# A convolution in fp16 halves: another order of the prologue, and the folds of unit 2 two streams earlier

## Chip, cores and metric

One core of one Trainium2 chip. The time is the device time of one execution in microseconds (us); lower is better. TensorE is called PE, VectorE DVE, ScalarE ACT, GpSimd POOL; SyncE is SP and only issues DMAs.

## What is computed

The input x has 32 images of 32 channels, 56 by 56 points, in float32. Each channel of each image is normalised by itself, then convolved with a 7 by 7 filter that is built from nine weighted points for each pair of channels; the bias and x itself are added.

```python
def construct_kernel(weight, P):            # weight (O, Cg, 9), P (2, Cg, 9)
    ph = clip(P[0], -3, 3) + 3;  pw = clip(P[1], -3, 3) + 3
    ih, iw = floor(ph), floor(pw);  rh, rw = ph - ih, pw - iw
    kern = zeros((O, Cg, 7, 7))
    for di, dj, frac in corners:            # four bilinear corners
        kern = kern.at[:, cidx, ih + di, iw + dj].add(weight * frac[None])
    return kern

def _gn(v):                                 # 32 groups of 32 channels: one channel each
    return (v - mean(v)) / sqrt(var(v) + 1e-5)

out = x + conv(_gn(x), construct_kernel(weight, P), padding=3) + bias
```

## The kernel before

Two images make a unit; there are 16 units. An image lies on 128 partitions as 32 channels times four groups of rows. All five engines run a list written out by hand; they meet through semaphores, and each engine takes its own list strictly in order.

**The prologue** builds the filter. PE turns the weights (L781) and gives the row of their maxima (L784). DVE builds `diag` and `cols` for three chunks (L591, L594), and PE multiplies them: three chunks of four products, in float32, 24 instructions at L819, into the pairs of banks `ps_eo` and `ps_x`. Two folds of the moments of unit 0 (`mean(0)`, `variance(0)`, L789) and one product that spreads the scales (L811) stand among them. The two halves of the filter are scaled into `kern`, one by DVE (L626), one by ACT (L400, `take_second_filters`); DVE adds filter parts (`filter_sum`, L617), and each of five parts is split into a high fp16 part by ACT (`filter_high`, L408, counted by `whi_ready`) and the rest by DVE (`filter_low`, L622, `wlo_ready`).

PE also multiplies zeros by zeros. Eight such dummies stand at the very start (L776). Eighteen more (`mark`, L827) come once `kern` is ready; they write the pairs `ps_x` and `ps_y`, so that later products add to what lies there, and the last one raises `marked`.

**Each unit** goes through the same steps. ACT sums its two images (`sums`, L314), PE folds the sums over partitions (`mean`), DVE takes `negmean` (L458), ACT sums the squares (`squares`, L322), PE folds those (`variance`), DVE takes `var` (`spread`, L464), ACT the root (L328), POOL five small steps for scale and offset (`newton_step`, L726 to L739). ACT normalises three groups of rows (L338) and POOL the last (L750). DVE forms differences (`odd_differences`, `differences`, `second_differences`, all L467). Nine streams, in six batches, are split into high (ACT, L352) and low fp16 parts (DVE, L490). After each third of the streams POOL copies them to other partitions with four DMAs (`shift`, L720, `xs` to `xb`). PE takes the streams in order (`convolve`, L855): for each up to 12 pairs of products, one from `xs` on one half of the array and one from `xb` on the other. The first `xb` product of streams 0, 3 and 6 waits for the shift of that third.

**Before stream 3** PE waits for `m11_ready`: ACT has copied the product of stream 0 (`middle`, L358). Before streams 4 and 7 it waits for seeds: ACT writes scaled points of x into `ps_x` and `ps_y` (`seed`, L368), and products are added to them. DVE combines the banks (`outs_0` to `outs_4`, L494), SP stores.

**Loads.** SP issues units 0 to 3 at the start, eight DMAs each (ACT issues four of unit 0). The load of unit u + 4 waits until both seeds of unit u and POOL's normalising of it are done, since they read the same buffer; then the store of unit u follows on the same queue.

From unit 1 on the order repeats (`step` of each engine). Unit 0 and the work on unit 1 beside it are written out: on ACT the list from `sums(0, 0, 0)` on, on DVE the list after L625, on PE `step(..., first=True)`, which folds the sums of unit 2 before stream 6 and its squares before stream 8.

Of the kernel before, what the change touches and what calls it, by code (L numbers as in the profile page):

```python
# [44 lines left out]
def build(nc, x, weight, P, bias, out):  # L45
# [8 lines left out]
    with ctx:  # L54
# [133 lines left out]
        def loaded(r, nth):  # L188

            return LOAD * nth + (LOAD // PER if r == 0 else LOAD)  # L190
# [107 lines left out]
        def _(act):  # L298
# [62 lines left out]
            def seed(u, r, k, first=False):  # L361

                if first:
                    act.wait_ge(marked, 1)
                else:
                    act.wait_ge(combined, OUTS * (u - 1) + (4, 7)[k])
                photo = xraw[:, PER * r:PER * (r + 1), :].rearrange("p m (n k) -> p m n k", k=4)[:, :, :, k::2]
                act.activation(pair_of((ps_x, ps_y)[k]).rearrange("p (n m) k -> p m n k", m=PER), photo,  # L368
                               ACT.Copy, scale=scales[:, 2:3]).then_inc(seeded, 1)
# [21 lines left out]
            sums(0, 0, 0)  # L391
            squares(0, 0)
            root(0)
            act.wait_ge(xn_zeroed, 6)
            normalise(0, 0, first=True)

            def take_second_filters():
                act.wait_ge(kern_in_psum, 4)
                act.wait_ge(scales_ready, 1)
                act.activation(kern[:, :, :, 1, :].rearrange("p j q (r o) -> p r (j q) o", r=2),  # L400
                               ps_x[:, :, 0:256].rearrange("p r (v o) -> p r v o", o=CH),
                               ACT.Copy, scale=scales[:, 0:1]).then_inc(kern_ready, 1)

# [5 lines left out]

            take_second_filters()  # L410
            act.wait_ge(edges_zeroed, 2)
            high(0, 0, *BATCHES[0], first=True)
            high(0, 0, *BATCHES[1], first=True)
            sums(1, 1, 0)
            filter_high(0)
            filter_high(1)
            squares(1, 1)
            high(0, 0, *BATCHES[2], first=True)
# [4 lines left out]
            filter_high(3)  # L423
            high(0, 0, *BATCHES[5], first=True)
            act.wait_ge(bias_loaded, DMA)
            middle(0, first=True)
            seed(0, 0, 0, first=True)
            normalise(1, 1, first=True)
            high(1, 1, *BATCHES[0], first=True)
            filter_high(4)  # L430
            sums(2, 2, 0)
            high(1, 1, *BATCHES[1], first=True)
            seed(0, 0, 1, first=True)
            squares(2, 2)
# [18 lines left out]
        def _(dve):  # L453
# [144 lines left out]
            dve.wait_ge(wmax_row, 1)  # L598
            dve.tensor_reduce(srow[:, 0:1], ps_y[0:1, 0, 0:CH], AX.X, ALU.max).then_inc(srow_step, 1)
            dve.wait_ge(srow_step, 1)  # L600
# [18 lines left out]
            def filter_low(n):  # L619
# [4 lines left out]

            dve.wait_ge(kern_in_psum, 2)  # L625
            dve.tensor_scalar(kern[:, :, :, 0, :].rearrange("p j q (r o) -> p r (j q) o", r=2),  # L626
                              ps_eo[:, :, 0:256].rearrange("p r (v o) -> p r v o", o=CH),
                              scales[:, 0:1], None, ALU.mult).then_inc(kern_ready, 1)
            odd_differences(0, 0)
            dve.wait_ge(kern_ready, 2)  # L630
            filter_sum(0, sums4[:, 0:2], kern[:, 0::2], kern[:, 1::2])
            low(0, 0, *BATCHES[0])
            low(0, 0, *BATCHES[1])
            dve.wait_ge(filt_summed, 1)
            filter_sum(2, sums4[:, 4:5], sums4[:, 0:1], sums4[:, 1:2])
            filter_sum(1, sums4[:, 2:4], kern[:, 0:2], kern[:, 2:4])
            mean(1, 1)
            filter_low(0)
            differences(0, 0)
            second_differences(0, 0)  # L640
            filter_low(1)
            spread(1)
            low(0, 0, *BATCHES[2])
# [5 lines left out]
            low(0, 0, *BATCHES[5])  # L649
            outs_0(0)  # L650
            odd_differences(1, 1)
            differences(1, 1)
            filter_low(4)
            low(1, 1, *BATCHES[0])
            low(1, 1, *BATCHES[1])
            outs_1(0)
            mean(2, 0)
            second_differences(1, 0)
            second_differences(1, 2)
            low(1, 1, *BATCHES[2])  # L660
            spread(2)
            low(1, 1, *BATCHES[3])
# [109 lines left out]
        def _(pe):  # L772

            pe.wait_ge(zeros_built, 1)
            for n in range(8):
                pe.matmul(ps_y[:, n % 2, 0:N], zeros[:, 0:128], zeros[:, 0:N], start=True, stop=True)  # L776
            pe.wait_ge(weights_loaded, DMA)
# [5 lines left out]
            pe.wait_ge(wmax_ready, 1)  # L783
            pe.matmul(ps_y[0:1, 0, 0:CH], wmax[:, :], ident[:, :], start=True, stop=True).then_inc(wmax_row, 1)  # L784

# [14 lines left out]
            def variance(u):  # L800
                pe.wait_ge(ssq_ready, u + 1)
                pe.wait_ge(var_ready, u)
                fold_columns(0, PER)

            pe.wait_ge(ones_built, 1)
            for k in range(CHUNKS):
# [6 lines left out]
                for n in range(4):  # L813
                    if k == 0 and n == 2:
                        pe.wait_ge(eye_built, 2 * GROUPS)
                        mean(0)
                    if k == 1 and n == 3:
                        variance(0)
                    last = pe.matmul((ps_eo, ps_x)[n // 2][:, n % 2, 0:256],  # L819
                                     diag[:, k, 4 * n:4 * n + 4, :].rearrange("p g c -> p (g c)"),  # L820
                                     cols[:, k].rearrange("p v o -> p (v o)"), start=k == 0, stop=k == CHUNKS - 1)
                    if k == CHUNKS - 1:
                        last.then_inc(kern_in_psum, 1)

            def mark(n):

                return pe.matmul((ps_x, ps_y)[n // 2 % 2][:, n % 2, 0:N], zeros[:, 0:128], zeros[:, 0:N],  # L827
                                 start=True, stop=True)

            pe.wait_ge(kern_ready, 2)  # L830
            pe.wait_ge(scales_ready, 1)
            for n in range(10):
                mark(n)
            mean(1)
            for n in range(8):
                last = mark(n)
            last.then_inc(marked, 1)
            variance(1)

            def convolve(u, par, s, nth):  # L840
# [20 lines left out]
            def step(u, par, nth, stats, first=False):  # L861
                for s in range(NS):
# [6 lines left out]
                    if first:  # L869
                        if s == 6:  # L870
                            mean(2)
                        if s == 8:
                            variance(2)
                    elif stats:
                        if s == 1:
                            mean(u + 2)
                        if s == 5:
                            variance(u + 2)
                    if s == 4:
                        pe.wait_ge(seeded, 2 * u + 1)  # L880
                    if s == 6:
# [30 lines left out]
```

## Time and profile before

| | us |
|---|---|
| median of 3 runs | 320.43 |
| lowest, highest | 318.5, 322.21 |
| profiled execution | 320.76 |
| its span | 318.9 |

The span runs from the first to the last instruction of the program, and the rows below count from its start. A row of the timeline merges instructions of one kind that follow each other: start, duration, engine, line, operation, tiles, shapes, count, and in brackets the idle time of the engine before it with what ended it. Ends of matmuls are modelled and overlap, so the pace is read from starts. A float32 product is two instructions.

### The profile page before, as it was taken

How to read it: one execution, taken by the hardware profiler on the slowest of the kernel's cores; microseconds unless marked ns; L12 is line 12 of the kernel's file. 1: busy time of each engine (PE TensorE's matmuls, PEld its weight loads, DVE VectorE, ACT ScalarE, POOL GpSimd, SP SyncE). 2: the span in 40 equal slices, each digit the busy share in tenths (PEclk: the TensorE clock that was granted, in tenths of full speed). 3: DMA queues.
4: the chain of work that ended last, by engine and by line, in shares of the span. 5: the costliest groups of instructions: out<-in, count | busy, mean ns of one | idle time of the engine just before them, and what ended most of it. 6: DMA issues, size and time to landing. Idle time of an engine off the chain costs nothing.

```text
span 318.9 us, 9740 instructions
## 1 busy us (share of the span) xinstructions
PE 294.9 (92%) x3452; PEld 204.2 (64%) x3452; DVE 267.3 (84%) x357; ACT 225.8 (71%) x328; POOL 177.6 (56%) x338
## 2 busy tenths in 40 slices
PE   5996798796999999999999999999999999999990
PEld 2653575574766767777767676777766677776760
DVE  4448896989998999999998989899999899996231
ACT  3368887878877797969796979878787869570300
POOL 6034938466665849393948566565748393944000
PEclk9999999999999999999999999999999999999998
DMA  8953369579999898989998999999998948488605
GB/s 142 151 115 90 98 162 190 133 166 219 236 207 241 189 261 171 257 177 236 206 238 180 233 201 219 224 219 234 194 253 178 260 98 237 98 233 222 141 2 102
DMA packets 128255, 59.09 MB, mean 185 GB/s; under 512 B 122068, under 2 KB 122068, under 8 KB 128228
## 3 DMA queue, kind: packets, MB, share of 16 engines
q1 hardware_dynamic: 115204, 24.90, 43.2%
q0 software_dynamic: 9312, 33.04, 39.3%
q10 hardware_dynamic: 3712, 0.80, 1.4%
q8 instruction: 14, 0.23, 0.3%
q14 instruction: 13, 0.11, 0.1%
HBM read 12.88 MB, written 12.85 MB: 81 GB/s over the span
## 4 chain that ended last, share of the span: by engine, by line
PE 66%; POOL 11%; DMA 8%; DVE 6%; issue 5%; ACT 2%; DVEq 0%; POOLq 0%; ACTq 0%
PE ps_eo L855 18%; PE ps_x L855 17%; PE ps_s L855 16%; PE ps_y L855 11%; DMA xb<-xs 7%; POOL xn L750 4%; POOL xb L720 3%; PE ps_eo L819 2%; DVE d L467 1%; POOL rtmp L726 1%; PE ps_x L819 1%; DVE xs L490 1%; DMA wnat<-L_conv_weight 1%; ACT xs L352 1%; PE ps_stat L789 1%
## 5 line engine op out<-in xcount | busy, mean ns | idle before, releaser
L720 POOL DMA_DIRECT2D xb<-xs x192 | 94.4, 498 | 55.0 <-DVE xs L490 51.9
L855 PE MATMUL ps_eo<-xs,w 128*64 128x392 f16 (+1 forms) x576 | 98.7, 325 | 0.0
L855 PE MATMUL ps_eo<-xb,w 128*64 128x392 f16 (+1 forms) x576 | 98.7, 324 | 0.0
L855 PE MATMUL ps_s<-xb,w 128*64 128x392 f16 (+1 forms) x384 | 68.2, 326 | 8.5 <-DMA xb<-xs 8.4
L855 PEld LDWEIGHTS ps_eo<-xb,w 128*64 128x64 f16 x576 | 61.6, 109 | 16.6
L855 PE MATMUL ps_s<-xs,w 128*64 128x392 f16 (+1 forms) x384 | 69.5, 326 | 1.8 <-ACT m L358 1.8
L855 PE MATMUL ps_x<-xb,w 128*64 128x392 f16 x384 | 67.6, 328 | 0.0
L855 PE MATMUL ps_x<-xs,w 128*64 128x392 f16 x384 | 67.6, 328 | 0.0
L855 PEld LDWEIGHTS ps_eo<-xs,w 128*64 128x64 f16 x576 | 61.7, 109 | 8.7
L490 DVE TENSOR_TENSOR xs<-e,xs 128x900 f16<-128x900 f32 x48 | 65.5, 1364 | 1.7 <-ACT xs L352 1.5
L352 ACT ACTIVATE xs<-e 128x900 f16<-128x900 f32 x48 | 58.9, 1226 | 8.9 <-DVE e L467 8.0
L855 PEld LDWEIGHTS ps_s<-xb,w 128*64 128x64 f16 x384 | 40.9, 109 | 25.1 <-DMA xb<-xs 11.8
L855 PEld LDWEIGHTS ps_x<-xb,w 128*64 128x64 f16 x384 | 40.8, 109 | 16.2
L855 PE MATMUL ps_y<-xs,w 128*64 128x392 f16 x288 | 50.6, 328 | 0.0
L855 PE MATMUL ps_y<-xb,w 128*64 128x392 f16 x288 | 50.6, 328 | 0.0
L750 POOL TENSOR_SCALAR xn<-xraw,scale,offset 32x784 f32<-32x784 f32 x32 | 46.4, 1458 | 1.7
L855 PEld LDWEIGHTS ps_s<-xs,w 128*64 128x64 f16 x384 | 41.0, 109 | 7.0 <-ACT m L358 2.1
L338 ACT ACTIVATE xn<-xraw,offset,scale 96x784 f32<-96x784 f32 x32 | 34.5, 1128 | 14.8 <-POOL offset L739 14.8
L726 POOL TENSOR_TENSOR rtmp<-rinv 128x2 f32<-128x2 f32 x16 | 13.6, 851 | 51.8 <-ACT rinv L328 51.8
L855 PEld LDWEIGHTS ps_x<-xs,w 128*64 128x64 f16 x384 | 40.8, 109 | 2.3
L855 PEld LDWEIGHTS ps_y<-xb,w 128*64 128x64 f16 x288 | 31.2, 109 | 11.7
L467 DVE TENSOR_TENSOR e<-d 128x900 f32<-128x900 f32 x32 | 34.0, 1107 | 0.0
(91 smaller groups left out, 459.3 us busy)
## 6 DMA issues: line engine op xcount, KB each, us to landing
xb<-xs POOLq DMA_DIRECT2D x96, 168.8 KB, 4.5
xb<-xs POOLq DMA_DIRECT2D x96, 166.9 KB, 4.7
xraw<-x SPq DMA_DIRECT2D x124, 98.0 KB, 3.2
out<-result SPq DMA_DIRECT2D x124, 98.0 KB, 4.8
xraw<-x ACTq DMA_DIRECT2D x4, 98.0 KB, 4.0
out<-result ACTq DMA_DIRECT2D x4, 98.0 KB, 3.7
wnat<-L_conv_weight POOLq DMA_DIRECT2D x1, 36.0 KB, 3.5
pts<-L_conv_P POOLq DMA_DIRECT2D x2, 1.1 KB, 3.1
```

Of the source, the lines that this page charges most:

```text
L338: act.activation(xn[0:96, r % 2, :, SLOTS * m + 1:SLOTS * m + 1 + ROWS, 1:1 + SIDE // 2], image(r, m)[0:96, :].rearrange("p (n w k) -> p k ...
L352: act.activation(halves(par, 0, s, count), stream(s, par, count), ACT.Copy).then_inc(hi_ready, count)
L467: dve.tensor_tensor(o, both(x0, shift), both(x1, 0), ALU.subtract).then_inc(differenced, 1)
L490: dve.tensor_tensor(halves(par, 1, s, count), stream(s, par, count), halves(par, 0, s, count), ALU.subtract).then_inc(lo_ready, count)
L720: pool.dma_start(dst[32 * g:32 * g + 32, 0:run - line * past], src[32 * f:32 * f + 32, line * past:run]).then_inc(shifted[par][b], DMA)
L726: pool.tensor_tensor(rtmp[:, :], rinv[:, :], rinv[:, :], ALU.mult).then_inc(newton, 1)
L750: pool.tensor_scalar(xn[96:128, u % 2, :, SLOTS * m:SLOTS * m + ROWS, 1:1 + SIDE // 2], image(u % RING, m)[96:128, :].rearrange("p (n w k) ...
L789: last = pe.matmul(ps_stat[p:p + HALF, a:b], eye[:, p:p + HALF], moments[:, a:b], start=True, stop=True)
L819: last = pe.matmul((ps_eo, ps_x)[n // 2][:, n % 2, 0:256], diag[:, k, 4 * n:4 * n + 4, :].rearrange("p g c -> p (g c)"), cols[:, k].rearra ...
L855: last = pe.matmul(into[p:p + HALF, :, 0:PER * wide], w[:, n // 2, s, q, t, :], moving.rearrange("p n q m -> p n (q m)"), start=fresh and ...
```

## The change

- PE: fourteen dummies at the start instead of eight; five more after the row of maxima, ahead of the filter; that row goes to `ps_stat`, no longer to `ps_y`. The fold of the squares of unit 0 also waits until DVE has read the row (`srow_step`). After the filter come the fold of unit 1's sums, two dummies that mark `ps_x`, twelve dummies into `ps_s`, the fold of unit 1's squares, eight more dummies. The folds of unit 2 stand before streams 5 and 7.
- ACT: the two sums of unit 1 stand around the root of unit 0, and the seed of `ps_y` of unit 0 before its normalising; the seed of `ps_x` stands behind the squares of unit 1. ACT no longer scales the second filter half. The normalising of unit 1 stands before `middle(0)`, `filter_high(4)` one place later.
- DVE scales both filter halves, adds two filter sums and takes `negmean` of unit 1 before the odd differences of unit 0; some later steps change places.
- SP's list is the same; the load of unit 4 waits for the seeds of unit 0, which now come before its streams.

```diff
             sums(0, 0, 0)
             squares(0, 0)
+            act.wait_ge(x_loaded[1], loaded(1, 0))
+            act.wait_ge(folded, mean_fold(0))
+            act.activation(junk[:, 1, 0, :], image(1, 0), ACT.Identity, accum_out=xsum[:, 0:1])
             root(0)
+            act.activation(junk[:, 1, 1, :], image(1, 1), ACT.Identity, accum_out=xsum[:, 1:2]).then_inc(sum_ready, 1)
+            seed(0, 0, 1, first=True)
             act.wait_ge(xn_zeroed, 6)
             normalise(0, 0, first=True)
...
-            take_second_filters()
             act.wait_ge(edges_zeroed, 2)
             high(0, 0, *BATCHES[0], first=True)
             high(0, 0, *BATCHES[1], first=True)
-            sums(1, 1, 0)
+            squares(1, 1)
             filter_high(0)
             filter_high(1)
-            squares(1, 1)
+            seed(0, 0, 0, first=True)
             high(0, 0, *BATCHES[2], first=True)
...
+            normalise(1, 1, first=True)
             act.wait_ge(bias_loaded, DMA)
             middle(0, first=True)
-            seed(0, 0, 0, first=True)
-            normalise(1, 1, first=True)
             high(1, 1, *BATCHES[0], first=True)
-            filter_high(4)
             sums(2, 2, 0)
             high(1, 1, *BATCHES[1], first=True)
-            seed(0, 0, 1, first=True)
+            filter_high(4)
             squares(2, 2)
...
-            odd_differences(0, 0)
+            for t, pair in enumerate((ps_eo, ps_x)):
+                dve.wait_ge(kern_in_psum, 2 * t + 2)
+                dve.tensor_scalar(kern[:, :, :, t, :].rearrange("p j q (r o) -> p r (j q) o", r=2),
+                                  pair[:, :, 0:256].rearrange("p r (v o) -> p r v o", o=CH),
+                                  scales[:, 0:1], None, ALU.mult).then_inc(kern_ready, 1)
             dve.wait_ge(kern_ready, 2)
             filter_sum(0, sums4[:, 0:2], kern[:, 0::2], kern[:, 1::2])
-            low(0, 0, *BATCHES[0])
-            low(0, 0, *BATCHES[1])
             dve.wait_ge(filt_summed, 1)
             filter_sum(2, sums4[:, 4:5], sums4[:, 0:1], sums4[:, 1:2])
+            mean(1, 1)
+            odd_differences(0, 0)
+            low(0, 0, *BATCHES[0])
             filter_sum(1, sums4[:, 2:4], kern[:, 0:2], kern[:, 2:4])
-            mean(1, 1)
+            low(0, 0, *BATCHES[1])
+            differences(0, 0)
             filter_low(0)
-            differences(0, 0)
+            spread(1)
             second_differences(0, 0)
             filter_low(1)
-            spread(1)
...
-            outs_0(0)
             odd_differences(1, 1)
             differences(1, 1)
+            outs_0(0)
+            low(1, 1, *BATCHES[0])
+            mean(2, 0)
+            low(1, 1, *BATCHES[1])
             filter_low(4)
-            low(1, 1, *BATCHES[0])
-            low(1, 1, *BATCHES[1])
             outs_1(0)
-            mean(2, 0)
             second_differences(1, 0)
+            spread(2)
             second_differences(1, 2)
             low(1, 1, *BATCHES[2])
-            spread(2)
...
-            for n in range(8):
-                pe.matmul(ps_y[:, n % 2, 0:N], zeros[:, 0:128], zeros[:, 0:N], start=True, stop=True)
+            for n in range(14):
+                pe.matmul((ps_x, ps_y)[n // 2 % 2][:, n % 2, 0:N], zeros[:, 0:128], zeros[:, 0:N],
+                          start=True, stop=True)
...
+            for n in range(5):
+                pe.matmul(ps_x[:, n % 2, 0:N], zeros[:, 0:128], zeros[:, 0:N], start=True, stop=True)
...
                     if k == 1 and n == 3:
+                        pe.wait_ge(srow_step, 1)
                         variance(0)
...
+            mean(1)
             pe.wait_ge(kern_ready, 2)
             pe.wait_ge(scales_ready, 1)
-            for n in range(10):
-                mark(n)
-            mean(1)
-            for n in range(8):
-                last = mark(n)
+            for n in range(2):
+                last = pe.matmul(ps_x[:, n, 0:N], zeros[:, 0:128], zeros[:, 0:N], start=True, stop=True)
             last.then_inc(marked, 1)
+
+            def warm(count):
+                for n in range(count):
+                    pe.matmul(ps_s[:, 0:N], zeros[:, 0:128], zeros[:, 0:N], start=True, stop=True)
+
+            warm(12)
             variance(1)
+            warm(8)
...
                     if first:
-                        if s == 6:
+                        if s == 5:
                             mean(2)
-                        if s == 8:
+                        if s == 7:
                             variance(2)
...
                     if s == 4:
-                        pe.wait_ge(seeded, 2 * u + 1)
+                        pe.wait_ge(seeded, 2 if first else 2 * u + 1)
```

## Rows read from the trace of the kernel before

**Rows 1.** The page, busy tenths of PE in 40 equal slices.

```profile
PE   5996798796999999999999999999999999999990
```

**Rows 2.** Waits of PE, 0 to 70 us: total, times, longest.

```profile
PE ps_s L855 <- DMA xb<-xs: 5.1, 3, 1.9
```

**Rows 3.** Timeline of PE, where it resumes in units 1 and 2.

```profile
50.88 0.35 PE L855 MATMUL ps_s<-xb,w 128*64 128x392 f16 x1 [1.53 <-DMA xb<-xs]
...
58.77 0.35 PE L855 MATMUL ps_s<-xs,w 128*64 128x392 f16 x1 [1.77 <-ACT m L358]
...
78.49 0.35 PE L855 MATMUL ps_s<-xb,w 128*64 128x392 f16 x1 [2.45 <-DMA xb<-xs]
```

**Rows 4.** Timeline of PE, the prologue and the start of unit 0.

```profile
1.20 2.79 PE L776 MATMUL ps_y<-zeros 128*128 128x392 f16 x8 [1.20 <-DVE zeros L558]
...
7.14 0.26 PE L784 MATMUL ps_y<-ident,wmax 32*1 32x32 f32 x2
8.52 2.05 PE L819 MATMUL ps_eo<-cols,diag 96*128 96x256 f32 x4 [1.13 <-DVE cols L594]
...
12.68 1.91 PE L819 MATMUL ps_eo<-cols,diag 96*128 96x256 f32 x4
14.39 1.06 PE L819 MATMUL ps_x<-cols,diag 96*128 96x256 f32 x2
...
19.22 1.91 PE L819 MATMUL ps_x<-cols,diag 96*128 96x256 f32 x4
21.91 0.83 PE L827 MATMUL ps_x<-zeros 128*128 128x392 f16 x2 [0.78 <-ACT kern L400]
...
24.50 0.86 PE L827 MATMUL ps_x<-zeros 128*128 128x392 f16 x2
...
26.05 0.49 PE L827 MATMUL ps_y<-zeros 128*128 128x392 f16 x2
26.38 0.49 PE L827 MATMUL ps_x<-zeros 128*128 128x392 f16 x2
...
30.16 0.35 PE L855 MATMUL ps_s<-xb,w 128*64 128x392 f16 x1 [1.67 <-DMA xb<-xs]
```

**Rows 5.** Timeline of DVE, 17 to 25 us.

```profile
19.54 0.75 DVE L626 TENSOR_SCALAR kern<-ps_eo,scales 128x512 f32<-128x512 f32 x1 [1.92 <-PE ps_eo L819]
20.20 1.08 DVE L467 TENSOR_TENSOR e<-xn 128x900 f32<-128x900 f32 x1
21.89 0.69 DVE L617 TENSOR_TENSOR sums<-kern 128x512 f32<-128x512 f32 x1 [0.60 <-ACT kern L400]
...
23.62 1.19 DVE L490 TENSOR_TENSOR xs<-e,xs 128x900 f16<-128x900 f32 x1 [0.45 <-ACT xs L352]
```

**Rows 6.** Timeline of ACT, 12.5 to 36 us.

```profile
12.91 0.19 ACT L322 ACTIVATION_READ_ACCUMULATOR junk<-xraw,negmean 128x1 f32 x1
...
17.78 2.07 ACT L338 ACTIVATE xn<-xraw,offset,scale 96x784 f32<-96x784 f32 x2 [1.58 <-POOL offset L739]
...
22.32 1.21 ACT L352 ACTIVATE xs<-e 128x900 f16<-128x900 f32 x1
23.38 0.84 ACT L314 ACTIVATE junk<-xraw 128x784 f16<-128x784 f32 x1
...
35.43 0.98 ACT L368 ACTIVATE ps_x<-xraw,scales 128x784 f32<-128x784 f32 x1
```

**Rows 7.** Windows: length; busy (count) of PE, PEld, DVE, ACT, POOL; PEclk, DMA, GB/s.

```profile
12.00:14.00 2.00, 2.00 (x7) 1.53 (x6) 0.80 (x8) 1.10 (x4) 0.00 (x0) 1.00 0.77 150
```

**Rows 8.** Waits of SP's queue, whole span: total, times, longest.

```profile
SPq L185 <- ACT ps_y L368: 23.0, 1, 23.0
```

**Rows 9.** Timeline of POOL, the first shifts of units 0 and 1.

```profile
25.42 2.03 POOL L720 DMA_DIRECT2D xb<-xs  x4 [5.57 <-DVE xs L490]
...
44.49 1.94 POOL L720 DMA_DIRECT2D xb<-xs  x4 [4.10 <-DVE xs L490]
```

**Rows 10.** Timeline of DVE, the variance of unit 2.

```profile
48.37 0.16 DVE L464 TENSOR_SCALAR var<-ps_stat 128x2 f32<-128x2 f32 x1
```

More of the change, by code:

```diff
@@ L363, in seed @@
                 if first:
-                    act.wait_ge(marked, 1)
+                    act.wait_ge(scales_ready, 1)
+                    if k == 0:
+                        act.wait_ge(marked, 1)
                 else:
@@ L392, in _ @@
             squares(0, 0)
+            act.wait_ge(x_loaded[1], loaded(1, 0))
+            act.wait_ge(folded, mean_fold(0))
+            act.activation(junk[:, 1, 0, :], image(1, 0), ACT.Identity, accum_out=xsum[:, 0:1])
             root(0)
+            act.activation(junk[:, 1, 1, :], image(1, 1), ACT.Identity, accum_out=xsum[:, 1:2]).then_inc(sum_ready, 1)
+            seed(0, 0, 1, first=True)
             act.wait_ge(xn_zeroed, 6)
             normalise(0, 0, first=True)
[L397 to L402, printed above, removed]
             def filter_high(n):
@@ L598, in _ @@
             dve.wait_ge(wmax_row, 1)
-            dve.tensor_reduce(srow[:, 0:1], ps_y[0:1, 0, 0:CH], AX.X, ALU.max).then_inc(srow_step, 1)
+            dve.tensor_reduce(srow[:, 0:1], ps_stat[0:1, 8:8 + CH], AX.X, ALU.max).then_inc(srow_step, 1)
             dve.wait_ge(srow_step, 1)
@@ L623, in filter_low @@
                                   ).then_inc(wlo_ready, 1)
[L625 to L628, printed above, removed]
-            odd_differences(0, 0)
+            for t, pair in enumerate((ps_eo, ps_x)):
[3 more added lines that the diff above has]
+                                  scales[:, 0:1], None, ALU.mult).then_inc(kern_ready, 1)
             dve.wait_ge(kern_ready, 2)
             filter_sum(0, sums4[:, 0:2], kern[:, 0::2], kern[:, 1::2])
-            low(0, 0, *BATCHES[0])
-            low(0, 0, *BATCHES[1])
             dve.wait_ge(filt_summed, 1)
             filter_sum(2, sums4[:, 4:5], sums4[:, 0:1], sums4[:, 1:2])
+            mean(1, 1)
+            odd_differences(0, 0)
+            low(0, 0, *BATCHES[0])
             filter_sum(1, sums4[:, 2:4], kern[:, 0:2], kern[:, 2:4])
-            mean(1, 1)
+            low(0, 0, *BATCHES[1])
+            differences(0, 0)
             filter_low(0)
-            differences(0, 0)
+            spread(1)
             second_differences(0, 0)
             filter_low(1)
-            spread(1)
             low(0, 0, *BATCHES[2])
@@ L783, in _ @@
             pe.wait_ge(wmax_ready, 1)
-            pe.matmul(ps_y[0:1, 0, 0:CH], wmax[:, :], ident[:, :], start=True, stop=True).then_inc(wmax_row, 1)
+            pe.matmul(ps_stat[0:1, 8:8 + CH], wmax[:, :], ident[:, :], start=True, stop=True).then_inc(wmax_row, 1)
             def fold_columns(a, b):
@@ L823, in _ @@
                         last.then_inc(kern_in_psum, 1)
-            def mark(n):
-                return pe.matmul((ps_x, ps_y)[n // 2 % 2][:, n % 2, 0:N], zeros[:, 0:128], zeros[:, 0:N],
-                                 start=True, stop=True)
+            mean(1)
             pe.wait_ge(kern_ready, 2)
             pe.wait_ge(scales_ready, 1)
-            for n in range(10):
-                mark(n)
-            mean(1)
-            for n in range(8):
-                last = mark(n)
+            for n in range(2):
+                last = pe.matmul(ps_x[:, n, 0:N], zeros[:, 0:128], zeros[:, 0:N], start=True, stop=True)
             last.then_inc(marked, 1)
+            def warm(count):
+                for n in range(count):
+                    pe.matmul(ps_s[:, 0:N], zeros[:, 0:128], zeros[:, 0:N], start=True, stop=True)
+            warm(12)
             variance(1)
+            warm(8)
             def convolve(u, par, s, nth):
```

## The prediction

> **What bounds the kernel now.** The page comes first: the busy digits of TensorE (PE) in forty slices of the span, of 8 us each, are full from the eleventh slice on, until the last [rows 1]. So an edit is worth what it changes before that, or what it moves the whole full stretch by. The waits of PE over the first 70 us say what is missing there: 5.1 us in three waits for the shifted copy xb [rows 2]; a fourth comes when unit 1 waits for its middle term m [rows 3], and a fifth, for a copy of unit 2, at 78.49 [rows 3]. Before unit 0, PE's timeline shows a burst of dummies, an idle piece, the small matmuls, the filter matmuls from 8.52, more dummies, and the first full pair of a stream at 30.16 [rows 4]. DVE waits for those filter matmuls, and again behind ACT's half of the filter [rows 5], so the filter stretch is on the path that sets the start.
>
> The profile's clock column reads 1.00 even where PE is slow [rows 7], so the level is read from the pace. Dummies of 392 columns go from 21.91 to 24.50, eight in 2.59 us, 0.324 each (1.2 GHz); from 26.05 two take 0.33 us, 0.165 each (2.4 GHz) [rows 4]. The filter instructions, four from 12.68 to 14.39, take 0.4275 each [rows 4]. By the order of the rows they lie between two stretches of low pace; I take them for low, and expect half of that, 0.214, at the high level. That no row shows a filter instruction at the high level is the largest unknown here.
>
> **The change, part by part.**
>
> *Dummies ahead of the filter.* Fourteen instead of eight, and five more after the row maximum: 14 times 0.324 is 4.5 us from 1.20 on, to 5.74, where the old burst of eight ended at 3.99 and was followed by idle time. In the later burst the high pace is there by 26.05, 4.1 us after its first dummy and after 0.78 us of idle time [rows 4]. The new first burst is longer than that, so I expect PE at 2.4 GHz when the five run. Would it stay there through the filter? The filter instructions at the low level did not raise it in 12.6 us; but once raised, it survived 1.67 us of idle time before 30.16 and 2.45 before 78.49 [rows 3, 4]. I take it as kept. The five cost 1.62 us from 7.40 at the low level, until 9.02, 0.5 past the old start; at the high level 0.83, until 8.23, hidden by the wait for cols that ends at 8.52 [rows 4].
>
> *Filter stretch.* From 8.52 to 21.13 it is 12.61 us: 24 instructions are 10.26, the rest, 2.35, two folds and one scale matmul with their breaks [rows 4]. At 0.214 to 0.255 each (the second is the weight load's own time: six in 1.53 us [rows 7]; I take 0.22) the 24 save 4.1 to 5.1 us, taken 5.0; of the breaks about a third, 0.8. The stretch ends near 15.3. The new wait of the second fold for srow_step costs nothing: what it waits for is read right after cols 2, and fold and filter come behind the squares anyway.
>
> Here the Trainium skill speaks against the change. The rows show weight load and matmul side by side: 2.00 us of PE and 1.53 of loading in one stretch of 2 us [rows 7]. "TensorE: Matmul & The Clock Gate", Part 3, "The mechanism", says that a weight load overlaps a running matmul only where the row groups differ; all filter loads use the same 96 rows. By that rule an instruction at the high level would take 0.214 plus 0.128 to 0.255, and the stretch would save 2.1 us or nothing. The overlap in the row disagrees with it at the low level.
>
> *Chain to the first shifted copy.* DVE now scales both filter halves: 15.3, plus kern 0.75, plus sum 0.69 (this length), a sum of half the size (0.4), mean 0.15 (both estimates, by size): 17.2. Then odd differences 1.08, ACT's high part 1.21, low part 1.19 [rows 5, 6]: 20.7, against 23.62 + 1.19 = 24.81 [rows 5], 4.1 earlier. This needs the normalised unit 0 at 17.2. Squares ended at 13.10 [rows 6]; their mean fold stands behind four filter instructions, so 1.0 earlier, 12.1. Then ACT does the first image sum of unit 1 (0.84 and its read, 0.95) to 13.0; the root and POOL's steps take about the 1.58 that ACT waits now plus 0.2, to 14.8; the second sum and the seed (0.98) fill that to 14.95; normalising, 2.07, ends at 17.0 [rows 6]. Just hidden: each us more there would cost a us. Sums that left the place after the high parts free ACT for the squares of unit 1.
>
> *Unit 4 loaded early.* SP sat 23.0 us behind the second seed of unit 0 [rows 8]. That seed now comes near 15, the other, behind the squares of unit 1 and two filter parts, near 23; SP's eight loads go out from there, no longer behind a seed in the middle of unit 0. SP has nothing else queued until unit 0's store. POOL's copies pay: from issue to PE's start 4.74 us without loads beside them (25.42 to 30.16), 6.39 with (44.49 to 50.88) [rows 3, 4, 9], so 1.65. The first copy meets half of them (0 to 1.65, taken 0.8), the second all; the first of unit 1 is freed. From the low part's end to PE it was 5.35: 20.7 + 5.35 + 0.8 = 26.9, so unit 0 starts 3.3 us earlier.
>
> *Folds of unit 2 at streams 5 and 7.* The variance of unit 2 was at 48.37 [rows 10], 18.2 us after unit 0's start. One stream earlier is 2.0 (12 pairs of 0.165), and the wait before stream 3 (1.9 at most [rows 2]) shrinks by about 1.0 (0 to 1.9), since its copy gets the 1.65 but its inputs come early: 26.9 + 18.2 - 3.0 = 42.1. ACT's root of unit 2 still stands behind the high part of stream 3, which hangs on DVE's second difference behind the mean's new wait: 0.7 lost (0 to 1.5). From there to unit 1's stream 3 it was 10.4 (48.37 to 58.77 [rows 3, 10]): 42.1 + 0.7 + 10.4 = 53.2, not 58.77. Later waits hang on the same chain and PE is full behind them, so the end moves by the same 5.6. The rest costs nothing that I can see: the row maximum goes to another bank, the last filter part (ACT and DVE) is needed by streams 7 and 8 alone, and the differences of unit 1 stand ahead of unit 0's first sum, which the banks of unit 1 need a unit later.
>
> **Sum.** The profiled execution took 320.76 us for a span of 318.9; the median of the runs is 320.43, 0.1% less. 320.76 - 5.6 = 315.2. With the bounds above (pace 0.9 worse; copies 0.8 either way; stall 1.0 and order 0.8 either way, not all at once) this case reaches from 313.6 to 317.0.
>
> **Rivals.**
>
> *Low clock through the filter: the change doesn't do what it says.* For it: 12.6 us of filter work never raised it [rows 4], and small matmuls part the bursts. Then the start is 0.5 late, ACT's loss of the second half puts kern, 0.75, behind 21.6, and the low part ends at 26.8, not 24.81; unit 0 starts near 32.3, 2.2 late. The folds give 2.0 of it back and the freed copy of unit 1 the rest: 321.2.
>
> *High clock, but the weight load shows.* If half of the 0.255 of a load can't be hidden, an instruction takes 0.214 + 0.128 = 0.34; the 24 save 2.1 and the breaks 0.5 instead of 5.8; the rest follows: 320.76 - 5.6 + 3.2 = 318.4. Against it: the overlap [rows 7]. The rule of the Trainium skill above is of this kind.
>
> *Slower: the first copy queued behind the filter and beside the loads.* The odd differences ran at 20.20, before the filter's last sums [rows 5]; now they stand behind both halves, two sums and a mean. At the low clock that is 3.0 us, and the loads of unit 4 then lie beside two copies of unit 0, 1.65 each. If the moved folds don't give it back, because root and high parts keep their old place in ACT's queue, 320.76 + 3.0 + 1.65 - 0.6 (a freed copy's part) = 324.8. It decides once the last filter matmul ends later than 17.2.
>
> *The clock falls again* in the idle pieces that the early filter opens: the marks and twelve dummies end near 18.4, the squares of unit 1, behind ACT's high part at 19.5, near 21.4; eight dummies end near 23, the copy is there at 26.9. These are 3.0 and 3.8 us, longer than the 2.45 that it survived [rows 3]. If the clock falls there, the first stream, 2.0 us, takes twice that; the waits ahead of streams 3 take up about half, which leaves about 1.0. It belongs to the forecast's range.
>
> **How the numbers follow.** Forecast 0.60; low clock 0.20; visible load 0.11; slower 0.09. Three runs spread by 1.2%, so about 1% is what can be told from no change (317.2 to 323.6 around 320.43). The forecast is faster by over 1%, low clock and visible load are within it, the last is slower; 0.61, 0.30, 0.09. The range that leaves out two in ten goes from 313.6 to 321.6.
>
> **What would show it.** Right: filter instructions about 0.21 to 0.25 apart, the last before 16; normalise ending before the first odd difference; unit 0's first full pair near 27, unit 1's stream 3 near 53; loads of unit 4 from about 23. Wrong: 0.4275 throughout, with the pair near 32; or a low first stream. The forecast fails most likely by the clock, next by the price of the loads beside the first two copies.

## The result, and the profile after

The changed kernel took 318.34 us in the median (18 runs, 315.52 to 323.23), the kernel before 320.07 (18 runs beside it). The ratio is 0.9925 [0.9897, 0.9953], so it is faster by 0.75%, where 1.6% was forecast. Medians here are of all runs, while ratios leave out those over 1.5% above the fastest of their kernel, which are six of the changed kernel's 18 (at mean clocks of 0.949 to 0.970) and none of the other's, so that this ratio flatters the change. Over all 18 the gain is 0.5% by the medians and 0.4% by the means. A second series gave 318.80 (10 runs, beside 321.06) and 0.9918 [0.9883, 0.9954]. The profiled execution of the changed kernel took 316.90 us, with a span of 315.1, against 320.76 and 318.9.

The page, as in [rows 1]: busy tenths of PE in 40 slices of 7.9 us, and under them the granted clock.

```profile
PE   8956997999999999999999999999999999999990
...
PEclk9995999799999999999999999999999999999998
```

The prologue is denser than in [rows 1], but the clock row has a 5 in the fourth slice and a 7 in the eighth. The timeline of PE, to be read against [rows 4] and [rows 3], shows what lies in them.

```profile
5.10 0.73 PE L774 MATMUL ps_x<-zeros 128*128 128x392 f16 x2
...
10.56 1.03 PE L822 MATMUL ps_eo<-cols,diag 96*128 96x256 f32 x4
11.43 0.59 PE L822 MATMUL ps_x<-cols,diag 96*128 96x256 f32 x2
...
14.10 1.03 PE L822 MATMUL ps_x<-cols,diag 96*128 96x256 f32 x4
...
21.75 0.28 PE L788 MATMUL ps_stat<-moments,eye 128*64 128x2 f32 x4 [3.28 <-ACT junk L322]
...
27.14 0.54 PE L858 MATMUL ps_s<-xb,w 128*64 128x392 f16 x1 [2.53 <-DMA xb<-xs]
...
27.47 0.53 PE L858 MATMUL ps_s<-xb,w 128*64 128x392 f16 x1
...
55.42 0.35 PE L858 MATMUL ps_s<-xs,w 128*64 128x392 f16 x1 [2.44 <-ACT m L358]
...
75.01 0.35 PE L858 MATMUL ps_s<-xb,w 128*64 128x392 f16 x1 [0.65 <-DMA xb<-xs]
```

Four filter instructions start from 10.56 to 11.43, 0.22 each, and the last four begin at 14.10: the filter stretch ends near 15.1 and no weight load shows. The first full pair stands at 27.14 (30.16 in [rows 4]), but the next one comes 0.33 later, which is the low pace. Of the three waits of [rows 3], the first is gone, the one at stream 3 of unit 1 has grown, and the one of unit 2 has shrunk. The windows (length; PE busy with its count; granted clock; DMA share; GB/s) show where the level fell.

```profile
20.00:22.00 2.00, 0.25 (x5) 1.00 0.66 131
22.00:24.00 2.00, 2.00 (x10) 0.66 0.58 140
...
28.00:30.00 2.00, 2.00 (x17) 0.50 0.81 187
...
34.00:36.00 2.00, 2.00 (x30) 1.00 0.94 241
...
58.00:60.00 2.00, 2.00 (x14) 0.50 0.61 121
```

The level is 1.2 GHz (0.50 in the clock column) from about 23 to 33 us, after the 3.28 us in which PE waited for the squares of unit 1, and again near 57 to 60, after the 2.44 us. DVE's timeline answers to [rows 5] and [rows 10]: filter halves scaled, low part, and the variance of unit 2.

```profile
14.38 0.75 DVE L624 TENSOR_SCALAR kern<-ps_eo,scales 128x512 f32<-128x512 f32 x1 [0.97 <-PE ps_eo L822]
...
17.49 1.09 DVE L464 TENSOR_TENSOR e<-xn 128x900 f32<-128x900 f32 x1
...
20.00 1.17 DVE L487 TENSOR_TENSOR xs<-e,xs 128x900 f16<-128x900 f32 x1 [0.28 <-ACT xs L352]
...
44.09 0.16 DVE L461 TENSOR_SCALAR var<-ps_stat 128x2 f32<-128x2 f32 x1 [0.20 <-PE ps_stat L788]
```

Up to the first pair the forecast holds within half a us (low part done at 21.2 against 20.7, pair at 27.14 against 26.9). The variance comes 2.0 late (42.1), stream 3 of unit 1 2.2 late (53.2).

### The profile page after: what moved, and what is told of

It reads as the page before. It is cut to its first block, busy times and chain, and to the rows that moved or that the text cites. A ratio compares the mean times of both kernels' runs of the same rounds, so it can differ in the third digit from the quotient of the medians.

```text
span 315.1 us, 9770 instructions
## 1 busy us (share of the span) xinstructions
PE 295.4 (94%) x3467; PEld 204.2 (65%) x3467; DVE 268.1 (85%) x358; ACT 224.3 (71%) x327; POOL 178.9 (57%) x338
## 4 chain that ended last, share of the span: by engine, by line
PE 69%; DMA 9%; POOL 8%; DVE 7%; issue 3%; ACT 1%; DVEq 0%; POOLq 0%; ACTq 0%
PE ps_eo L858 21%; PE ps_s L858 17%; PE ps_x L858 17%; PE ps_y L858 11%; DMA xb<-xs 8%; POOL xn L748 3%; DVE xs L487 3%; POOL xb L718 2%; DVE e L464 1%; DMA wnat<-L_conv_weight 1%; DVE result L491 1%; PE ps_eo L822 1%; PE ps_x L822 1%; POOL rtmp L724 1%; PE ps_stat L788 1%
## 5 line engine op out<-in xcount | busy, mean ns | idle before, releaser
L858 PE MATMUL ps_eo<-xs,w 128*64 128x392 f16 (+1 forms) x576 | 99.8, 327 | 0.0
L858 PE MATMUL ps_eo<-xb,w 128*64 128x392 f16 (+1 forms) x576 | 99.7, 326 | 0.0
L858 PE MATMUL ps_s<-xb,w 128*64 128x392 f16 (+1 forms) x384 | 70.7, 334 | 3.9 <-DMA xb<-xs 3.9
L858 PE MATMUL ps_s<-xs,w 128*64 128x392 f16 (+1 forms) x384 | 71.7, 334 | 2.4 <-ACT m L358 2.4
L858 PE MATMUL ps_x<-xs,w 128*64 128x392 f16 x384 | 68.7, 332 | 0.0
L858 PE MATMUL ps_x<-xb,w 128*64 128x392 f16 x384 | 68.7, 332 | 0.0
L858 PEld LDWEIGHTS ps_s<-xb,w 128*64 128x64 f16 x384 | 42.0, 111 | 20.3 <-DMA xb<-xs 6.5
L858 PEld LDWEIGHTS ps_s<-xs,w 128*64 128x64 f16 x384 | 42.0, 111 | 9.4 <-ACT m L358 2.8
L322 ACT ACTIVATE junk<-xraw,negmean 128x784 f16<-128x784 f32 x32 | 30.1, 942 | 5.6 <-DVE negmean L455 5.4
```

What stands on the lines that cost most here:

```text
L322: last = act.activation(junk[:, r % 2, m, :], image(r, m), ACT.Square, bias=negmean[:, r % 2, m:m + 1], accum_out=ssq[:, m:m + 1])
L858: last = pe.matmul(into[p:p + HALF, :, 0:PER * wide], w[:, n // 2, s, q, t, :], moving.rearrange("p n q m -> p n (q m)"), start=fresh and ...
```

## The experiments

The theory after the first look (the clock theory): the steps are right, and what is missing is TensorE's level, which falls in the idle pieces that the change opens. Rivals: the price of unit 4's loads beside two copies (the loads theory), and the worth of the moved folds.

**The changed kernel again**, unchanged, beside the other experiments.

> The changed kernel once more, for its spread on this chip and another profiled execution. Clock theory: 315.5 to 323 us, each run's time following its mean granted clock; if the clock is low in this profile in the filter or the first streams, the first full pair or unit 1 come later by that. Rival: a run at a mean clock of 0.98 is no faster than one at 0.955.

318.80 us. Its profiled execution took 322.36 us, though it is the same program. The windows of PE, with columns as above:

```profile
4.00:6.00 2.00, 1.06 (x6) 1.00 1.20 243
6.00:8.00 2.00, 1.95 (x12) 0.86 1.37 196
8.00:10.00 2.00, 2.00 (x6) 0.50 1.26 175
...
34.00:36.00 2.00, 2.00 (x16) 0.50 1.08 260
```

and its timeline of PE:

```profile
3.79 0.61 PE L774 MATMUL ps_x<-zeros 128*128 128x392 f16 x2
...
12.48 1.91 PE L822 MATMUL ps_eo<-cols,diag 96*128 96x256 f32 x4
14.19 1.06 PE L822 MATMUL ps_x<-cols,diag 96*128 96x256 f32 x2
...
32.66 0.54 PE L858 MATMUL ps_s<-xb,w 128*64 128x392 f16 x1 [3.48 <-DMA xb<-xs]
```

Here the dummies reached the high pace near 4 us, the level fell again before 8, and the filter ran at 0.43 per instruction (four from 12.48 to 14.19), as before the change. The first pair is 5.5 us later than in the other execution, and the time is 5.5 us longer. So the step that gives the change its gain holds in some executions and not in others. Over the 28 runs of both series the time follows the mean granted clock that stands beside each: correlation -0.84, 313.1 us + 190 us times (1 - clock) by least squares, clocks from 0.949 to 0.983. (A stretch at the low level costs half its length if PE would not have waited anyway, and lowers the mean by half its share of the 315 us span; fully paid, the slope would be 315. 190 says that about 60% is paid.) The profile of the kernel before shows a mean of 0.995 although its first 26 us went at the low pace [rows 4], so the mean counts low stretches only after the first rise. It is therefore not compared with that of the kernel before, whose 69 runs beside the experiments show no such relation (+0.33).

**Low filter**: the first rival of the prediction by itself, with the dummies ahead of the filter as before the change.

```diff
-            for n in range(14):
+            for n in range(8):
...
-            for n in range(5):
-                pe.matmul(ps_x[:, n % 2, 0:N], zeros[:, 0:128], zeros[:, 0:N], start=True, stop=True)
```

> The changed kernel with eight dummies at the start and none ahead of the filter, as before the change, so that the filter runs at the low level. Clock theory: filter instructions 0.4275 us apart, unit 0 starts near 32, 320.5 to 322.5 us, no faster than the kernel before. Rival (the moved steps alone bring the gain): 317 to 319 us.

321.69 us (10 runs), ratio 1.0030 [0.9993, 1.0066], as the clock theory expected. The rival had priced it at 321.2 with the first pair near 32.3; in the timeline of PE the filter is at the low pace and the pair comes at 32.43:

```profile
12.68 1.91 PE L819 MATMUL ps_eo<-cols,diag 96*128 96x256 f32 x4
14.39 1.06 PE L819 MATMUL ps_x<-cols,diag 96*128 96x256 f32 x2
...
32.43 0.35 PE L855 MATMUL ps_s<-xb,w 128*64 128x392 f16 x1 [3.06 <-DMA xb<-xs]
```

Without the high level in the filter the new order gains nothing that can be told. Whether the dummies alone would gain as much in the old order is open: no run has them there.

**Loads of unit 4 held** until unit 0 has combined two streams.

```diff
-            with sp.Fori(0, UNITS // RING - 1) as it:
+            for u in range(RING):
+                sp.wait_ge(combined, 2)
+                sp.wait_ge(seeded, 2 * u + 2)
+                sp.wait_ge(last_group_normalised, NORMS * u + NORMS)
+                load(u + RING, u)
+                store(u, u % 2)
+            with sp.Fori(1, UNITS // RING - 1) as it:
```

> The changed kernel with the loads of unit 4 held until the second combined sum of unit 0 (near 43 us), as late as they were before. Clock theory: the first copy lands up to 0.8 us earlier, the one of stream 3 up to 1.65 earlier behind a slow first stream that hides it, the first of unit 1 up to 1.65 later; 317.5 to 319.5 us. Loads theory: the lost gain comes back, 315 to 316.5 us.

320.49 us (316.30 to 324.32, 10 runs), ratio 0.9915 [0.9873, 0.9956]; the median of the kernel before beside it is 320.80. The loads theory had expected 315 to 316.5: it falls. The clock theory's 317.5 to 319.5 was missed too, and these ten times don't follow their mean clock (0.01), so why the median is 2 us above the changed kernel's stays open. Its windows of PE:

```profile
26.00:28.00 2.00, 0.00 (x0) 0.50 0.36 121
28.00:30.00 2.00, 1.25 (x8) 0.50 0.01 3
```

its first copy on POOL's timeline and first pair on PE's:

```profile
22.95 2.02 POOL L724 DMA_DIRECT2D xb<-xs  x4 [5.27 <-DVE xs L493]
```

```profile
28.75 0.54 PE L864 MATMUL ps_s<-xb,w 128*64 128x392 f16 x1 [3.50 <-DMA xb<-xs]
```

and the first copy of the changed kernel:

```profile
21.77 2.03 POOL L718 DMA_DIRECT2D xb<-xs  x4 [5.27 <-DVE xs L487]
```

The first pair came at 28.75, later than the 27.14 of the changed kernel, but its first filter instructions were low, so its copy was also issued 1.18 later (22.95 against 21.77). From issue to pair it took 5.80 us with the loads held (the DMA share was 0.36 and 0.01 from 26 to 30 us), against 5.37 with them (0.80 and 0.81): holding the loads did not shorten this copy.

**No fill**: no dummies between the marks and unit 0's streams.

```diff
-            warm(12)
             variance(1)
-            warm(8)
```

> The changed kernel without any dummies between the marks and the first stream. Clock theory: the clock falls no later than in the changed kernel and stays low for as long or longer, mean granted clock 0.95 to 0.975, 318.5 to 321 us. Loads or folds theory: these dummies don't matter, about 318.3 us.

317.89 us (316.92 to 320.77, 4 runs), ratio 0.9905 [0.9871, 0.9939]: the clock theory's 318.5 to 321 was missed in the median. Twenty dummies, too few to hold the level, are worth nothing that four runs can tell. In its profiled execution (320.77 us) the level had fallen by 10 us and the filter ran at 0.43, as in the repeated one.

**Fill**: enough dummies to leave no idle time there.

```diff
-            warm(12)
+            warm(30)
             variance(1)
-            warm(8)
+            warm(27)
```

> The changed kernel with 30 and 27 dummies around the fold of unit 1's squares, instead of 12 and 8, so that TensorE has work from the marks to the first stream. Clock theory (the clock fell in the idle pieces that the early filter opened, and that took back most of the gain): the granted clock stays at 1.00 from 22 to 34 us, the first full pair comes near 27.1 as in the changed kernel, unit 1 starts near 44.6, stream 3 of unit 1 near 53; about 314.9 us, ratio 0.983, and a narrower spread of the runs. Loads or folds theory (the early loads, or the waits behind the moved folds, took it back): the streams of unit 0 run faster, but the next wait grows by as much; about 318, as the changed kernel.

318.07 us (12 runs), ratio 0.9917 [0.9879, 0.9956]: no better in the median, where the clock theory had expected 314.9 and its rival 318. Seven of the 12 runs lie at 317.0 to 318.2 with a mean clock of 0.986 to 0.989, four at 320.9 to 323.4 with 0.959 to 0.966, and one at 324.2 with 0.982, which the mean clock doesn't explain. The profiled one (317.90), in its timeline of PE:

```profile
9.09 1.67 PE L822 MATMUL ps_eo<-cols,diag 96*128 96x256 f32 x4
10.69 0.28 PE L788 MATMUL ps_stat<-moments,eye 128*64 128x2 f32 x4
10.90 1.13 PE L822 MATMUL ps_x<-cols,diag 96*128 96x256 f32 x4
...
54.87 0.54 PE L858 MATMUL ps_s<-xs,w 128*64 128x392 f16 x1 [2.39 <-ACT m L358]
...
77.22 0.35 PE L858 MATMUL ps_s<-xb,w 128*64 128x392 f16 x1 [3.49 <-DMA xb<-xs]
```

It shows both halves of why: unit 0 ran at the high level throughout, but all nineteen dummies ahead of the filter and its first instructions were low, and the level fell at 55 us after 2.39 us of waiting for `m`. It did not fall behind the longer wait of 3.49 us in unit 2 (28 matmuls from 78 to 80 us at a clock of 1.00).

**Folds of unit 2 back** before streams 6 and 8 (`if s == 5` and `if s == 7` become 6 and 8), the rest as changed.

> The changed kernel with the folds of unit 2 before streams 6 and 8 again (the order of the vector engine's list stays as changed). Clock theory: the folds are worth what the sum gave them, one stream: 1 to 2.5 us slower than the changed kernel, 319.5 to 321 us. Folds theory (they only made the vector engine and ScalarE wait): no slower, 316 to 318.3 us.

324.11 us (320.11 to 327.54, 10 runs), ratio 1.0058 [1.0022, 1.0094], outside what either theory expected. It looks as if the folds were worth over 5 us. But its profiled execution (324.34) had a low filter, and against the repeated changed kernel, also with a low filter (322.36), it is 2.0. So the folds had to be priced again where the level is kept (below).

**Dense**: the fill, and 17 and 8 dummies ahead of the filter instead of 14 and 5.

```diff
-            for n in range(14):
+            for n in range(17):
...
-            for n in range(5):
+            for n in range(8):
...
-            warm(12)
+            warm(30)
             variance(1)
-            warm(8)
+            warm(27)
```

> The changed kernel with 17 dummies at the start and 8 ahead of the filter (14 and 5 in the change), and 30 and 27 dummies after it, so that TensorE has no idle piece but the small matmuls until the first stream. Clock theory (the gain comes and goes with the level that TensorE is granted in the prologue and the first units; over the 18 runs of the changed kernel the time follows the mean granted clock, and meets 313.2 us at 1.00): the filter runs at the high level in nearly all executions, mean granted clock 0.98 or more, median 315 to 316.5 us, few runs over 319. Rival (the spread has another cause, such as the transfers beside the copies): median and spread stay as with the changed kernel, 318 us and 316 to 323.

315.71 us (314.38 to 316.91, 6 runs), ratio 0.9825 [0.9789, 0.9861]: what was forecast for the change. As six runs were few, it ran again:

> The dense version a second time (17 and 8 dummies ahead of the filter matmuls, 30 and 27 between the marks and unit 0's streams). Clock theory: TensorE keeps its level through the filter and unit 0 in nearly all executions, so the times stay between 314 and 317.5 us, the median near 315.7, ratio 0.980 to 0.986. Rival, that the first six runs were lucky draws of the same mixture as the changed kernel's: several runs between 318 and 322, median near 318, ratio near 0.992.

316.75 us (314.14 to 320.06, 11 runs), ratio 0.9888 [0.9855, 0.9921]. The second series is less good and missed what was expected of its median and ratio; but only one of the 17 runs lies above 317.4 us, and their median is 316.45. The time again follows the clock (0.981 to 0.995): 312.6 us + 337 us times (1 - clock), so now low stretches seem to be paid about in full (without the one run above 319 the slope is 273). The line meets that of the changed kernel at the clock of 1 within half a us, and the six runs at 0.990 or above have a mean of 315.4. The first profiled execution, windows:

```profile
22.00:24.00 2.00, 1.68 (x13) 1.00 0.51 110
...
28.00:30.00 2.00, 2.00 (x30) 1.00 0.77 161
...
54.00:56.00 2.00, 1.69 (x12) 0.59 0.45 134
```

and timeline of PE, where it resumes in unit 1 and unit 2:

```profile
54.31 0.54 PE L858 MATMUL ps_s<-xs,w 128*64 128x392 f16 x1 [2.44 <-ACT m L358]
...
75.50 0.35 PE L858 MATMUL ps_s<-xb,w 128*64 128x392 f16 x1 [2.25 <-DMA xb<-xs]
```

The filter and unit 0 are at the high level; the wait for `m` remains, and the level falls behind it (0.54 instead of 0.35 for the first product). In the second series' profile it survived the 2.44 us there and fell behind the 2.07 us of unit 2.

**Early dummies only**: 17 and 8 ahead of the filter, 12 and 8 as changed behind it.

> Only the denser dummies ahead of the filter (17 and 8); 12 and 8 between the marks and the streams, as in the changed kernel. If both idle places count: the filter is at the high level in nearly all runs and the first streams of unit 0 fall in most, median 316.5 to 317.5, between the changed kernel (318.3) and the dense one (315.7). If the early dummies do it all: 315 to 316.5. If they do nothing, and the later fill does it all: 318 to 319.

317.07 us (315.09 to 318.40, 6 runs), ratio 0.9897 [0.9851, 0.9944]: between changed and dense, as expected if both places count, but it can't be told from the dense series beside it. In its profile the filter is at the high level and the first streams are not.

**Dense, and twelve dummies in unit 1's wait** ahead of stream 3 (into `ps_x`, and the seed of unit 1 waits for them).

```diff
+                    if isinstance(u, int) and u == 1 and k == 0:
+                        act.wait_ge(marked, 2)
...
+                    if s == 3 and isinstance(u, int) and u == 1:
+                        pe.wait_ge(combined, 4)
+                        for n in range(12):
+                            last = pe.matmul(ps_x[:, n % 2, 0:N], zeros[:, 0:128], zeros[:, 0:N], start=True, stop=True)
+                        last.then_inc(marked, 1)
```

> As the dense one, and twelve dummies more before stream 3 of unit 1, where TensorE sat idle for 2.4 us and the clock fell behind it; they go into the pair that unit 0 has read, and the seed of unit 1 waits for them. Clock theory: no fall near 56 us, another 1 to 2 us less, 313.5 to 315.5 us, mean granted clock 0.985 or more. Rival: no change from the dense one.

317.74 us (314.59 to 318.46, 6 runs), ratio 0.9869 [0.9818, 0.9919]: no gain on dense, and the clock theory's 313.5 to 315.5 was missed. Windows of its profiled execution:

```profile
54.00:56.00 2.00, 1.84 (x22) 1.00 0.36 118
...
72.00:74.00 2.00, 0.00 (x0) 1.00 1.08 236
74.00:76.00 2.00, 1.61 (x10) 0.60 1.16 219
```

The fall at 54 is gone, and the level falls at 74 instead, behind the next wait (2.96 us). Two runs at a clock of 0.993 took 314.6 and 315.0, four at 0.986 took 317.5 to 318.5.

**Dense, with the folds back** before streams 6 and 8.

> The dense version with the folds of unit 2 back before streams 6 and 8, to price the folds where the clock is kept. The prediction's price, 2.0 us for a stream and up to 1.0 of the wait: 317.7 to 318.7. A full price as first measured on the changed kernel (324.1 against 318.6): 320.5 to 322. If that first difference was mostly the clock, which had fallen in the filter of that profile: 316 to 317.5.

317.58 us (316.15 to 318.54, 7 runs), ratio 0.9910 [0.9875, 0.9945]: 0.8 us above dense in the same series, less than the price, and not clear of noise (the intervals overlap). The timeline of PE of this kernel, where it resumes in units 1 and 2,

```profile
56.04 0.35 PE L858 MATMUL ps_s<-xs,w 128*64 128x392 f16 x1 [1.86 <-ACT m L358]
...
75.15 0.35 PE L858 MATMUL ps_s<-xb,w 128*64 128x392 f16 x1 [1.84 <-DMA xb<-xs]
```

and of dense, second series:

```profile
54.07 0.35 PE L858 MATMUL ps_s<-xs,w 128*64 128x392 f16 x1 [2.44 <-ACT m L358]
...
73.41 0.38 PE L858 MATMUL ps_s<-xb,w 128*64 128x392 f16 x1 [2.07 <-DMA xb<-xs]
...
73.92 0.53 PE L858 MATMUL ps_s<-xs,w 128*64 128x392 f16 x1
74.24 0.53 PE L858 MATMUL ps_s<-xb,w 128*64 128x392 f16 x1
```

with its windows:

```profile
72.00:74.00 2.00, 0.59 (x6) 0.90 1.18 245
74.00:76.00 2.00, 2.00 (x16) 0.50 1.01 214
76.00:78.00 2.00, 2.00 (x22) 0.75 1.20 258
```

The folds move the variance by 1.97 (44.70 against 42.73 on DVE's timeline), the stream by 1.97 and the copy of unit 2 by 1.74 us, near the price. But dense then waits longer (2.44 and 2.07 against 1.86 and 1.84) and is at the low pace just after 73.41 (starts 0.32 apart at 74), where the windows of the kernel with the later folds show none. These low stretches add up to some 3.4 us, which costs 1.7, and the lead of 1.74 is gone at the end: the spans are 314.6 and 314.3. At the same mean clock of 0.992 two dense runs of the first series took 315.1 and 315.4, four with late folds 316.1 to 317.8. By the rows the order is worth its 2 us up to unit 2, and the clock takes some or all of them back.

## Why the prediction was off

**The step that failed** is "I take it as kept", in the paragraph on the dummies ahead of the filter, together with the paragraph "The clock falls again", which allowed for one fall of 1.0 us within the range. With more dummies, so that the level mostly holds (dense), the kernel took 315.71 and 316.75 us, near the forecast's 315.2; as changed it took 318.34. The runs show three places where the level is lost.

- *Ahead of the filter.* With 14 and 5 dummies three profiled executions of six ran the filter low (the repeated one, no fill, folds back), two rose inside it (fill, held loads), and one kept it high. In four of the five the level had been raised and was lost between 7.3 and 9.2 us by their windows; in fill the dummies never raised it, so there the sentence before ("I expect PE at 2.4 GHz when the five run") failed too. With 17 and 8 all five profiled executions kept the filter high. It cost 5.5 us in the one pair of executions that differ by little else (316.90 against 322.36). The prediction had this as a rival with a chance of 0.20, one for the whole kernel; it is a share of the executions of every such kernel.
- *Unit 0's first streams.* With twelve and eight dummies the level fell there in all six profiled executions; with 30 and 27 it stayed high there in all five. The mechanism and the price stood in the prediction, after waits of 3.0 and 3.8 us (3.28 and 2.53 in the rows after). It cost 1.1 to 1.4 in the variance of unit 2 (44.09 against 42.98 and 42.73), near the 1.0. Early dummies alone show that it can also cost nothing there: with the level at 0.50 until 30 us the variance was at 42.83; the wait ahead of stream 3 of unit 0, 0.97 and 1.21 us in dense, does not show in its rows, so the slow stream seems to have taken its place.
- *Behind the waits of units 1 and 2.* Not foreseen, because waits of 1.77 and 2.45 us had done no harm in [rows 3]. Behind a wait for `m` of 2.39 to 2.53 us at stream 3 of unit 1 the level fell in seven of nine profiled executions (kept after 2.44 in the second dense one and after 2.53 with the folds back). Some ten pairs at the low pace (54.31 to about 57.5 in dense) are 10 times 0.165, 1.65 us each time.

**Term by term**, first pair, variance of unit 2, stream 3 of unit 1, copy of unit 2, span (us, from the timelines):

| | pair | var | stream 3 | copy | span |
|---|---|---|---|---|---|
| before | 30.16 | 48.37 | 58.77 | 78.49 | 318.9 |
| forecast | 26.9 | 42.1 | 53.2 | | 313.3 |
| changed | 27.14 | 44.09 | 55.42 | 75.01 | 315.1 |
| dense, second | 27.20 | 42.73 | 54.07 | 73.41 | 314.6 |
| dense, late folds | 27.05 | 44.70 | 56.04 | 75.15 | 314.3 |
| low filter | 32.43 | 48.70 | 60.04 | 79.86 | 319.9 |

(The forecast's span is 318.9 - 5.6.) The filter's pace (0.22), its end (15.3 against 15.1), the chain to the low part (20.7 against 21.2), the first pair, and the folds (2.0) were right. With the level kept, stream 3 of unit 1 came 0.9 late: 0.3 stands at the first pair already, and the terms for the wait before stream 3 of unit 0 and for the order of ACT's queue were 0.3 and 0.2 too good. The 0.8 for loads beside the first copy is not shown: the copy took 0.63 longer from issue to pair than before (5.37 against 4.74), but 1.06 longer where the loads were held. "Later waits hang on the same chain" holds only in part: from stream 3 to the copy of unit 2 it is 19.1 to 19.8 us in the five measured rows of the table, but up to 22.4 in the other profiled executions (fill), and the end moved by 4.3 where stream 3 had moved by 4.7 (dense, second).

**The weight load.** The rival of the visible load, 0.34 per instruction, is out: 0.22 was measured at the high level (10.56 to 11.43). "TensorE: Matmul & The Clock Gate" of the Trainium skill, Part 3, "The mechanism", has loads overlap only where the row groups differ, though its first paragraph also lets a load into a background weight buffer go ahead. These loads use the same 96 rows throughout, and the trace disagrees with the first rule at both levels: from 12 to 14 us PE was busy for 2.00 us and loads ran for 1.53 at the low level [rows 7] and for 1.56 at the high one. The slower rival needed a filter that ends late; the executions that had one took 320.8 to 324.3 us, near the 324.8 only where the folds were late too. The sum of the low-clock rival was slightly off: its terms put the low part at 27.1, not 26.8, and the pair at 32.4, where the low filter had 32.43.

**What stays open.** Why one execution keeps its level where the next one loses it. The same program raised it near 4.0 us in one execution and after 5.1 in another, and only the first lost it before the filter; but no fill and folds back, with the same dummies up to there, also raised it after 5.1 and lost it at 8.6 and 9.2 us. "TensorE: Matmul & The Clock Gate" of the Trainium skill, Part 1, "What's actually happening", says that the number of matmuls before the rise differs between runs of one kernel; the rows agree (the fill's fourteen dummies saw no rise at all). The mean clock is not the whole account either: the times follow it in the changed kernel, in fill (-0.75) and in dense (-0.90), but not with held loads (0.01), a low filter (0.20) or late folds (-0.36, and +0.64 in dense). Also open is why late folds cost over 5 us in the median of the kernel as changed: 2.0 are theirs, and its mean clock (0.965 against 0.970) explains about 1 more by the line of 190 us.

## What to carry to other kernels

A stretch that gains from TensorE's high level gains only in the executions that have it: price it as a share of runs, and put dummies where idle time is, before and after, as long as the times show a gain: here they paid ahead of the filter, ahead of unit 0 their gain could not be told (317.07 us with the few, 316.75 with the many, in one series), and in unit 1's wait they only moved the fall to the next one. When waits are shortened ahead of a full engine, look at the waits that then grow, because an engine that waits longer may also be slow when it resumes (0.54 instead of 0.35 for a product behind 2.44 us). Price an order of work between executions of the same clock: two medians of kernels whose level is lost by chance showed over 5 us, and 0.8 with the level better kept, for a step whose rows show 2.0.

## What was not expected of the hardware

- The longest wait is not the one that loses the level. It was lost after 2.07 us (second dense profile) and after 2.44 (first), and kept after 2.44 (second), after 2.45 [rows 3] and even after 3.49 (fill, 77.22).
- Two profiled executions of one program differed by 5.5 us (316.90 and 322.36) by where the level was lost.
- The filter products ran at either level, and some 12 us of them could pass without a rise: in the repeated execution they stayed at 0.50 with PE busy for 2.00 of 2.00 us (8 to 10 us above), in the first they kept the high pace throughout. In fill and with held loads the level rose while they ran (in fill four took 1.60 us from 9.09, and the next four 0.97 from 10.90).
